# Attention and LayerNorm on one core: fp32 scores in 64x32 tiles over two key halves, 32x32 block transposes, P times V in four 64x64 tiles

## What is computed

```python
x_seq = x.reshape(B, S, d_model)                      # B 16, S 900, d_model 512
q, k, v = proj(wq, bq), proj(wk, bk), proj(wv, bv)    # B, 8, 900, 64
scores = einsum('bhqd,bhkd->bhqk', q, k) / sqrt(64)
scores = scores + spatial_bias_matrix(...)            # by |dh| + |dw| of two tokens
attn = softmax(scores, axis=-1)
ctx = einsum('bhqk,bhkd->bhqd', attn, v)
resid = ctx.reshape(B, S, 512) @ wo + bo + x_seq
out = layernorm(resid) * ln_gamma + ln_beta
```

## Time and profile before

| | |
|---|---|
| median of 3 runs | 4176.31 us (4156.1 to 4186.96) |
| span of the profiled execution, first to last instruction | 4168.2 us |
| busy, of the span | PE 95%, PEld 78%, DVE 67%, ACT 59%, POOL 15% |
| DMA engines | mean 55 GB/s |

### The profile page before, as it was taken

The page is one execution under the profiler, slowest core; times in us unless marked ns, Lnnn a source line. Parts: engine busy times, 40 slices in busy tenths (PEclk is TensorE's granted clock), DMA queues, the critical chain, the costliest instruction groups (busy, mean ns, idle before and its releaser), DMA issues.

```text
span 4168.2 us, 74488 instructions
## 1 busy us (share of the span) xinstructions
PE 3974.2 (95%) x26624; PEld 3254.2 (78%) x26624; DVE 2776.1 (67%) x5393; ACT 2443.8 (59%) x4742; POOL 644.4 (15%) x648
## 2 busy tenths in 40 slices
PE   3999999999999999999999999999999999999998
PEld 3888878788787877878778787787877878788786
DVE  3676757667576775767767676675766757667676
ACT  2674746647466474655746557465674756747464
POOL 0003012030110302103021030200203012030113
PEclk8999999999999999999999999999999999999999
DMA  5121211212121121212211122111221111211111
GB/s 141 39 61 47 57 43 56 62 51 60 44 57 53 55 57 54 56 43 65 59 47 55 39 69 56 49 51 45 63 62 48 54 45 56 62 51 56 47 53 46
DMA packets 119844, 230.45 MB, mean 55 GB/s; under 512 B 15336, under 2 KB 57320, under 8 KB 119416
## 3 DMA queue, kind: packets, MB, share of 16 engines
q1 hardware_dynamic: 99657, 157.40, 14.3%
q10 hardware_dynamic: 19760, 67.51, 5.0%
HBM read 131.65 MB, written 33.92 MB: 40 GB/s over the span
## 4 chain that ended last, share of the span: by engine, by line
PE 82%; ACT 7%; DMA 5%; issue 3%; DVE 3%; SPq 1%; POOL 0%; DVEq 0%; POOLq 0%; ACTq 0%
PE pv_ps L629 18%; PE s_ps L592 16%; PE t_ps L606 16%; PE spare_ps L542 9%; PE pv_ps L542 5%; PE spare_ps L569 4%; PE pv_ps L555 4%; PE spare_ps L555 4%; PE pv_ps L569 4%; ACT prob L709 3%; ACT prob_t L727 2%; DMA wqk_sb<-wqk_split 2%; DMA tokens<-in_x 1%; ACT q_sb L699 1%; DMA bias_by_w<-bias_grid 1%
## 5 line engine op out<-in xcount | busy, mean ns | idle before, releaser
L727 ACT ACTIVATE prob_t<-t_ps 120x480 f32<-120x480 f32 x1920 | 993.2, 571 | 799.2 <-PE t_ps L606 798.4
L592 PE MATMUL s_ps<-k_sb,q_sb 128*120 128x450 f32 (+2 forms) x4096 | 1031.0, 376 | 84.2 <-DVE q_sb L832 45.0
L709 ACT ACTIVATE prob<-prob,row_min 120x900 f32<-120x900 f32 (+1 forms) x960 | 1009.5, 1052 | 39.4 <-DVE row_min L853 33.1
L853 DVE CUSTOM_DVE_ANT_0 prob<-s_ps,window 120x900 f32<-120x900 f32 x896 | 975.6, 1089 | 35.0 <-PE s_ps L592 29.5
L606 PE MATMUL t_ps<-ident,prob 120*120 120x120 f32 x7680 | 962.2, 268 | 10.5 <-DVE prob L866 10.1
L606 PEld LDWEIGHTS t_ps<-ident,prob 120*120 120x120 f32 x7680 | 830.2, 137 | 176.5 <-issue 56.9
L629 PE MATMUL pv_ps<-prob_t,values 120*64 120x240 f32 x8192 | 853.5, 362 | 26.5 <-ACT prob_t L727 20.8
L592 PEld LDWEIGHTS s_ps<-k_sb,q_sb 128*120 128x120 f32 (+2 forms) x4096 | 705.5, 180 | 188.6 <-issue 80.5
L629 PEld LDWEIGHTS pv_ps<-prob_t,values 120*64 120x64 f32 x8192 | 594.6, 140 | 268.7 <-issue 85.3
L866 DVE TENSOR_SCALAR prob<-prob,row_inv 120x900 f32<-120x900 f32 (+1 forms) x960 | 765.8, 798 | 33.8
L542 PE MATMUL spare_ps<-xt,wqk_sb 128*128 128x450 f32 x2112 | 524.2, 380 | 0.0
(11 more groups left out here) (73 smaller groups left out, 2934.3 us busy)
## 6 DMA issues: line engine op xcount, KB each, us to landing
wqk_sb<-wqk_split ACTq DMA_DIRECT2D x126, 512.0 KB, 3.8
k_sb<-k_sb SPq DMA_DIRECT2D x252, 225.0 KB, 3.4
tokens<-in_x SPq DMA_DIRECT2D x212, 240.0 KB, 3.0
out<-tokens SPq DMA_DIRECT2D x105, 240.0 KB, 2.4
tokens<-in_x SPq DMA_DIRECT2D x30, 120.0 KB, 3.2
wqk_split<-k_sb SPq DMA_DIRECT2D x8, 256.0 KB, 3.7
wqk_split<-ctx_t SPq DMA_DIRECT2D x8, 256.0 KB, 3.9
out<-tokens SPq DMA_DIRECT2D x15, 120.0 KB, 1.9
```

The source lines that it names most:

```text
L592: last = pe.matmul(s_ps[0:n, u % 2, half, 0:HALF], q_sb[:, p % 2, head, q0:q0 + n], k_sb[:, p % 2, head, part, half * HALF:half * HALF + H ...
L709: nc.scalar.activation(prob[0:n, u % BUFS, 0:S], prob[0:n, u % BUFS, 0:S], ACT.Exp, scale=-1.0, bias=row_min[0:n, s:s + 1], accum_out=row_ ...
L727: nc.scalar.activation(dst, src, ACT.Copy).then_inc(moved, 1)
L853: nc.vector.tensor_tensor_reduce(halves(prob[0:n, u % BUFS, 0:S]), s_ps[0:n, u % 2, :, 0:HALF], halves(bias.rearrange("p a c -> p (a c)")) ...
```

## The change

The whole kernel is laid out anew; the work computed stays the same.

- **Unit.** A unit is now two image rows of queries (2 x 30, each padded to 32) of a pair of heads: again 15 for a pair, 60 for an image, 960 in all. Partition 64a + 32r + w holds query w of image row a against key half r (450 keys); the two heads lie side by side.
- **Scores** take plain fp32 q and k (no split): 8 matmuls a unit, each 64 rows by 32 weight columns by 450 columns, on 8 different tiles of the array. Two units are issued together, 6 units ahead (`AHEAD`).
- **Softmax** is done for each key half by itself; a row's minimum and sum go to the partner partitions by 4 small transfers for two units (SP), and POOL, ACT, POOL and DVE work out the factor that joins them (`leads`, `ratios`, `totals`, `weights`). `normalise` moves from DVE to POOL. The bias-and-minimum operation and exp are now two operations of 450 for a unit instead of one of 900.
- **Transposes** on PE and their copies on ACT are gone: `turn` (DVE) transposes 32x32 blocks of 128 x 960 elements in one operation for each unit.
- **P times V**: a group is 4 units (3 at the end of a pair), 16 for an image. 15 blocks x 2 image rows x 2 heads = 60 fp32 matmuls of 64 rows, 64 weight columns and 120 columns (90 at the end of a pair), on four tiles.
- **Background**: pieces, values and output tiles keep their 12 matmuls each. Pieces are moved by one ACT operation over 128 partitions, with no DVE part. Values pass through DRAM (`stage`, `v_dram`) to get the new layout; bv goes through wo into bo. Context is kept in fp32 and split by POOL (`split_context`) tile by tile. The steps are placed anew (`place`): up to 8 steps (24 matmuls) in an even unit, 2 steps where a group of P times V runs. Two banks `r_ps` take them in turn.

```diff
-AHEAD = 3
+AHEAD = 6
+RING = 6
+PV_UNITS = [4, 8, 12, 16, 20, 24, 28, 30, 34, 38, 42, 46, 50, 54, 58, 60]
+XT_UNITS = [30, 30, 32, 32, 34, 34, 36, 36]
+SPLIT_UNITS = [0, 0, 4, 7, 8, 11, 14, 16]
+EARLY = [("piece", 1, 2), out(0), ("piece", 1, 3), out(1), out(2), out(3), ("piece", 2, 0), out(4), ("piece", 2, 1),
+         out(5), ("piece", 2, 2), out(6), ("piece", 2, 3), out(7)] + pieces(3)
+PV_STEPS, FULL_STEPS = 2, 8
...
+            def exchange(im, x):
+                s = x // 2 % STATS
+                sp.wait_ge(exp_done, 2 * im.unit(x + 2))
+                for a in range(4):
+                    c = a ^ 1
+                    sp.dma_start(other[QUAD * a:QUAD * a + QUAD, s, :, :], own[QUAD * c:QUAD * c + QUAD, s, :, :]
+                                 ).then_inc(exchanged[s], 16)
...
+            def scores(im, u):
+                if not known(unit, 1):
+                    pe.wait_ge(scores_min, 2 * (unit - 1))
+                for a in range(2):
+                    q0 = GRID * (2 * v + a)
+                    for r in range(2):
+                        row = 2 * QUAD * a + QUAD * r
+                        for head in range(2):
+                            d = slice(DK * head, DK * head + DK)
+                            last = pe.matmul(s_ps[row:row + QUAD, u % 2, head, 0:HALF], q_sb[d, p % 2, q0:q0 + QUAD],
+                                             k_sb[d, p % 2, columns(r)], start=True, stop=True, skip_group_check=True)
-            def transposes(im, u):
...
+            def context(im, g):
+                pe.wait_ge(turned, im.unit(PER_PAIR * p + PER_GROUP * gi + n))
+                for j in range(BLOCKS):
+                    for a in range(2):
+                        half = slice(2 * QUAD * a, 2 * QUAD * a + 2 * QUAD)
+                        for head in range(2):
+                            d = slice(DK * head, DK * head + DK)
+                            last = pe.matmul(pv_ps[d, a, 0:n * GRID].rearrange("d (u w) -> d u w", u=n),
+                                             values[half, p % 2, j, d],
+                                             prob_t[half, g % 2, 0:n, head, QUAD * j:QUAD * j + GRID],
+                                             start=(j == 0), stop=(j == BLOCKS - 1), skip_group_check=True)
...
+            def body(im, u):                                   # ACT
+                if im.live(u + AHEAD):
+                    exponentials(im, u + AHEAD)
+                if u % 2 and im.live(u + 3):
+                    ratios(im, u + 3)
+                ...
+                for work in im.evicted(u):
...
+            def turn(im, u):                                   # DVE
+                dve.wait_ge(prob_done, 2 * im.unit(u) + 2)
+                nc.vector.transpose(out=prob_t[:, g % 2, v % PER_GROUP, :, :].rearrange("p h k -> p (h k)"),
+                                    in_=prob[:, u % RING, :, :].rearrange("p h k -> p (h k)")).then_inc(turned, 1)
+            def body(im, u):                                   # DVE
+                if im.live(u):
+                    turn(im, u)
+                if u % 2 == 0 and im.live(u + 2):
+                    weights(im, u + 2)
+                if im.live(u + AHEAD):
+                    biased_scores(im, u + AHEAD)
...
+            def normalise(im, u):                              # POOL
+                pool.wait_ge(weight_done, im.b * (UNITS // 2) + u // 2 + 1)
+                for head in range(2):
+                    nc.gpsimd.tensor_scalar(prob[:, u % RING, head, 0:HALF], prob[:, u % RING, head, 0:HALF],
+                                            weight[:, s, c:c + 1], None, ALU.mult).then_inc(prob_done, 1)
+            def body(im, u):                                   # POOL
+                if u % 2 == 0 and im.live(u + 2):
+                    totals(im, u + 2)
+                if im.live(u + 2):
+                    normalise(im, u + 2)
+                if u % 2 and im.live(u + 3):
+                    leads(im, u + 3)
+                for work in im.out_tiles(u - 2):
+                    scale_shift(im, work)
+                for work in im.out_tiles(u - 1):
+                    reciprocal_std(im, work)
+                for work in im.out_tiles(u + 1):
+                    add_bias(im, work)
+                for t in range(NT):
+                    if SPLIT_UNITS[t] == u and not im.first:
+                        split_context(im, ("out", t))
```

More of the change, by code:

```diff
@@ L47 @@
 EPS = 1e-5
 BIG = 3.0e38
+CLAMP = 80.0
 PARTS = 3
 TERMS = [(0, 0), (0, 1), (1, 0)]
[L51 to L70 removed]
@@ new lines, in bank_of, with wanted @@
+def bank_of(item):
+    if item[0] in ("first_xt", "final"):
+        return item[1] % 2
+    if item[0] == "bv_wo":
+        return 0
+    return BANK[item]
+def wanted(item, first, last):
+    if item[0] == "out":
+        return not first
+    if item[0] in ("xt", "value") or item[0] == "piece" and item[1] >= PAIRS:
+        return not last
+    return True
+def background(u, first, last):
+    work = [("xt", t, 0, KT) for t in range(NT) if XT_UNITS[t] == u and not last]
+    work += [(*item, k0, k1) for item, k0, k1 in STEPS.get(u, []) if wanted(item, first, last)]
+    if last:
+        work += [("final", t, 0, KT) for t in range(NT) if FINAL_UNITS[t] == u]
+    return work
@@ new lines, in order, with evicted, out_tiles @@
+def order(first, last):
+    return [w[:-2] for u in range(END) for w in background(u, first, last) if w[-1] == KT]
+def evicted(u, first, last):
+    items = [("xt", t) for t in range(NT) if XT_UNITS[t] + 1 == u and not last]
+    items += [item for item in SEQUENCE if EVICT.get(item) == u and wanted(item, first, last)]
+    if last:
+        items += [("final", t) for t in range(NT) if FINAL_UNITS[t] + 1 == u]
+    return items
+def out_tiles(u, first, last):
+    return [w for w in evicted(u, first, last) if w[0] in ("out", "final")]
@@ new lines, in _ @@
+            for t in range(NT):
+                work_on(pro, ("first_xt", t))
+            for work in pieces(4):
+                work_on(pro, work)
+            pe.wait_ge(cleared, 3)
+            def body(im, u):
+                if u % 2 == 0:
+                    for x in (u + AHEAD, u + AHEAD + 1):
+                        if im.live(x):
+                            scores(im, x)
+                if u < 0:
+                    for work in PROLOGUE_STEPS.get(u, []):
+                        work_on(pro, work)
+                    return
+                if u == 0 and not im.first:
+                    context(Before(im), GROUPS - 1)
+                g = group_at(u)
+                if g is not None:
+                    context(im, g)
+                for work in im.background(u):
+                    work_on(im, work[:-2], *work[-2:])
@@ L664, in _ @@
             images(pe, body)
-            end = Image(B - 1, last=True)
-            context(end, GROUPS - 1, end.uses_before_unit(UNITS, 1))
-            for work in background(UNITS, False, True):
-                out_tile(end, UNITS, work)
         @block.scalar
```

1148 lines of the change are left out of this document (573 added, 575 removed).

## The result

The changed kernel took 4873.4 us (median of 4 runs, 4869.4 to 4877.1), the kernel before 4171.6 beside it: a ratio of 1.168, interval 1.163 to 1.172. The forecast was 3790 with a range up to 4330, so it had the wrong sign, and the time is outside the range.

What follows compares the result with a forecast made beforehand. PE (6.7 us) and DVE (6.9) nearly tie per double unit, but POOL's 8.6 bounds the first 13: 112 + 121 = 233 us an image. Fourteen images, first, last, start and end give 3790 us, own range 3450 to 3950, wider range 3430 to 4330.

Steps and rivals of the forecast that it cites:

- fp32 reading: PE matmuls: each instruction costs 2 x 0.83 ns a column on its tile, divided by the tiles that run together.
- issue rival: PE: starting instructions binds; at 83 ns each, 11.2 us a double unit, some 5300 us in all; chance 0.08.
- Fewer tiles at once: PE scores: four tiles at once instead of eight, about 4290 us, chance 0.10; one at a time, over 6000, chance 0.05.
- Transposes dearer: DVE's `turn`: 2.1 us each, double units of 8.5 and 9.3, about 4300 us; chance 0.08.
- exchange that is not covered: SP's small transfers: `leads` waiting for one would show it; each double unit would lose up to 3 us.
- DVE's wait for the chain: DVE before `weights`: exp, `ratios`, `totals` and four hops, some 2.0 us a double unit, of which `turn` covers 1.1.
- price of `normalise`: POOL, 450 elements: 0.65 us each, between a cheap bound of 0.47 and a dear bound of 1.16.
- POOL dearer: POOL: `normalise` at 1.16 us, an image 262 us, about 4220 us, nothing won; decides from 1.0 us; chance 0.12.
- waits around the banks: PE waiting for ACT's move, about 1.2 us, or the x tiles, 4 us: together 10 us an image.
- the clock: PE: granted clock 0.988 in the kernel before, upper level nearly all the time, no clock to win back.
- Filling ends near 97: Start of the kernel: 6 units of filling with all value tiles end near 97 us.

Runs made afterwards that it cites:

- e9: Changed kernel with `normalise` left out, evictions (x tiles included) placed first and POOL's bias addition to the residual at the start of its body: 3847.7 us.
- e10: Order of e9 with all of the computation, `normalise` of one head on POOL in two-operand form, the other on ScalarE: 3980.8 us, ratio 0.954 to the kernel before.
- e1: Changed kernel with POOL's `normalise` multiplying by a constant instead of the per-row factor: 4731.4 us.
- e2: Changed kernel with POOL's `normalise` as a two-operand product, the factor broadcast along the row: 4267.7 us.
- e3: Changed kernel with the `normalise` multiplications left out, POOL only posting its signals: 4039.7 us.
- e11: e10 with one statement moved on DVE, `weights` behind `biased_scores`: 3888.4 us, ratio 0.935 to the kernel before.
- e5: e3 with k, q and value evictions ahead of ACT's exponentials and DVE's output projection addition ahead of the transposes, in units without x tiles: 4021.9 us.

## Why the prediction was wrong

**What PE does was right.** The fp32 reading carried over. In the changed kernel an instruction of the scores took 538 ns (median; "some 540"), two units 1.74 us ("about 1.7") with eight tiles at once, a group of P times V of 120 instructions 3.31 us ("about 3.1"). The issue rival is out: the trace has 3.31 us for 120, 28 ns each. The Trainium skill (TensorE: Matmul & The Clock Gate, Step-by-step: what each phase is for) gives about 62 ns for each MATMUL where the sequencer's own code handles it, and the prediction worked out a total near 4500 from that; the matmuls of this trace come twice as fast. "Fewer tiles at once" is out as well.

**DVE and ACT were right.** `turn` 1172 ns (1.15), `biased_scores` 0.62 + 0.08 us, an exponential 0.665 + 0.187. "Transposes dearer" is out.

**Transfers were right in the changed kernel, and only there.** Each landed in 1.7 us (bound 3.4), and POOL waited for the exchange 91 us in all, 86.5 of them once at the start. But the prediction's own sign of an exchange that is not covered, `leads` waiting for a transfer, shows as soon as POOL is light. The changed kernel, then e9:

```profile
POOL lead L1015 <- DMA other<-own: 91.3, 4, 86.5
```

```profile
POOL lead L1015 <- DMA other<-own: 1382.3, 365, 86.9
```

SP issues the four transfers one after the other, in 1.9 us. By the traces' times, from the end of a double unit's last exponential to the landing of its last transfer are 4.4 us in the changed kernel and 5.0 in e9 (means over images 2 to 13), not the 3.4 of one transfer. In the changed kernel `leads` started 6.2 us after the landing, in e9 1.1. From the last exponential to `weights` e9 and e10 take 9.7 us, half of it this exchange. The prediction had about 2.0 for DVE's wait for the chain and took the exchange for covered; no run made it shorter, so what it costs is open.

**The step that failed first: the price of `normalise`.** "I take 0.65", with bounds of 0.47 and 1.16; it is 1.43. The rival "POOL dearer" named the place and the mechanism, and gave it 0.12. (Its "decides from 1.0 us on" does not come out of its sum: with 4 x the price + 1.7 the late double units pass the forecast's 6.9 at 1.3 us.) With 1.43 in that sum the late double units come to 5.7 + 1.7 = 7.4 (they are 7.6) and the first thirteen to 7.4 + 4.3 = 11.7 (they are 11.5). The same sum gives the first thirteen of e1 11.4 (11.2 measured) and those of e2 9.8 (9.9). So the mechanism was right to some 3%, and the term was mis-sized by 0.78 us. By this sum it is worth 49 of the 64 us lost in an image. The error is in the bound: it was read from rows of another form, on the belief that one operand must be cheaper than two, which no row supported. The rows of before had memset and select at 1.6 and 2.3 ns a column, start included, without any sign of whether a multiplication would follow either; e1 has 3.0.

**The step that failed second: the waits around the banks.** The prediction gave them 10 us an image, of which 4 for the x tiles, as a property of the bank itself: ACT needs 1.2 us to move a tile. What PE waited for was not the move but its place in ACT's and DVE's queues, behind exponentials, transposes and `weights`, which in turn wait for PE, POOL and a transfer. Without `normalise` an image should have taken 30 x 6.9 + 4 = 211 us by the prediction's numbers; e3 took 245.8. Of these 35 us, 12 came back with the order of the evictions and the residual (e9). That e9 then stands at 233.8, the forecast's 233, is chance: it does no `normalise`. Another 6 came back, from e10 to e11, with the place of `weights`. The double units with x tiles keep about 8.5 us against 7.4 (8.3 in e5 to 8.6 in e10); no run here changed that, and values placed a unit later were not tried.

**Third, and not in the sum: the clock.** The prediction costed PE at 0.988 throughout, since the trace of before had it, though it forecast a PE with gaps. The same 52744 matmuls took 3515.7 us at a clock of 0.857 and 3296.8 in e9 at 0.938. Those 219 us are not idle time but busy time, longer at the lower clock. How much of them reached the kernel's time no run tells, since POOL set the pace of the changed kernel.

**Fourth, small: the start.** "Filling ends near 97": the first `turn` is at 128.9 us. PE waited 34.4 us, until 81.0, for DVE's `wv_sb`, and DVE 45.5 for ACT's, so that the eight value tiles start only there; behind them PE does two pieces (7.6 us) and the product of bv and wo (3.6), for which DVE waits 16.6 us ahead of the first `turn`.

Together: the start and the first image cost 81 us more than forecast, fourteen images 64.2 each or 898, the last image and the end 102; that is the 1081 us between the two spans.

Open is why the one-operand form is so slow on this engine (e1 leaves 1353 ns with no factor to read), and how much of e11's remaining 236 us an image against 211 is the clock at 0.928, how much the exchange and the chain behind it, and how much the waits for banks.

## What to carry to other kernels

Before moving an elementwise operation to GpSimd, get a price for exactly that form (one operand or two, its length), for a bound from another form is none; here a rewrite of the same multiplication with a broadcast second operand took 605 us off the kernel. Price a bank or buffer wait not by the length of the move that frees it but by what stands ahead of that move in its engine's queue; when an operation is moved to the front, read the next trace for what it now waits for, as e5 traded 137 us of one wait for 251 of another. And once a change gives TensorE gaps, its busy time can grow too (3516 us at a clock of 0.857, 3297 at 0.938 for the same matmuls): cost a part of it by rows at the lower clock. An exchange that a slow engine covers must be costed again, issue and landing together, once that engine is fast.

## What the runs showed of the hardware that I had not expected

- GpSimd, 450 fp32 elements in each of 128 partitions: multiplication by a per-row factor 1430 ns, by a constant 1353, by a broadcast second operand 939. ScalarE took 657 for it and VectorE 480.
- VectorE's block transpose of fp32 keeps the pace of an ordinary operation: 1172 ns for 960 elements, against 624 for `biased_scores` with 450, which is 1.07 ns for each further element.
- Small fp32 matmuls on packed tiles start closer together than I had dared to assume on this chip: 28 ns apart in P times V, with durations that overlap (shortest 234, median 262 ns).
